# Seven row gathers ahead and nine behind the first jobs, and scale columns read through a register instead of tables

## The reference, cut to what matters

```python
def _L0_xattn_ref(hidden_states, token_ids, Wg, Wu, Wd):
    expert_ids = jnp.minimum(tid // tokens_per_expert, E - 1)
    for e in range(E):
        g = jax.nn.silu(jnp.einsum('bsd,fd->bsf', hidden_states, Wg[e]))
        u = jnp.einsum('bsd,fd->bsf', hidden_states, Wu[e])
        y = jnp.einsum('bsf,df->bsd', g * u, Wd[e])
        out = jnp.where((expert_ids == e)[..., None], y, out)
...
x = x + jnp.tanh(g_xattn[0]) * _L0_xattn_ref(_layernorm(x, axis=-1), itok_BxS_13_99985, ctx_2048, ctx_2048, ctx_2048)
x = x + jnp.tanh(g_ffn[0]) * _L0_ffn_ref(_layernorm(x, axis=-1), L0_ffn_weight)
```

## Time and profile before

| | |
|---|---|
| median of 3 runs | 201.29 us (201.24 to 203.76) |
| the profiled execution: its own time | 201.43 us |
| its span | 199.7 us |
| PE busy | 144.3 us, 72% |
| DVE busy | 156.3 us, 78% |
| ACT busy | 112.7 us, 56% |
| POOL busy | 81.8 us, 41% |

### The profile page before, as it was taken

One profiled execution on the slowest core, in us unless ns is written; L12 is line 12 of the kernel. 1 busy time (PEld: TensorE's weight loads), 2 busy tenths in 40 slices (PEclk: granted clock), 3 DMA queues, 4 the chain that ended last, 5 costly groups with the idle time before them and its releaser, 6 DMA issues.

```text
span 199.7 us, 3062 instructions
## 1 busy us (share of the span) xinstructions
PE 144.3 (72%) x723; PEld 69.7 (35%) x727; DVE 156.3 (78%) x351; ACT 112.7 (56%) x166; POOL 81.8 (41%) x117
## 2 busy tenths in 40 slices
PE   0141939998999797999998999999851266566600
PEld 0110424443555343544444445555420223223200
DVE  2876697798758799899989787776686999998820
ACT  2366596887524854688868534233313987666510
POOL 7158787320312344332386673001110023566670
PEclk9999996999999999999999999999997579999985
DMA  0937998200000222111212210000000002132351
GB/s 6 365 113 198 355 408 264 85 2 0 0 3 0 54 56 53 26 39 43 54 26 53 56 26 0 3 0 2 0 5 0 0 0 105 57 153 113 149 208 59
DMA packets 15440, 15.68 MB, mean 79 GB/s; under 512 B 10816, under 2 KB 11328, under 8 KB 15424
## 3 DMA queue, kind: packets, MB, share of 16 engines
q1 hardware_dynamic: 12576, 7.09, 11.8%
q0 software_dynamic: 2560, 8.39, 11.6%
q10 hardware_dynamic: 288, 0.00, 0.1%
HBM read 8.92 MB, written 4.19 MB: 66 GB/s over the span
## 4 chain that ended last, share of the span: by engine, by line
PE 38%; DVE 33%; issue 11%; POOL 7%; ACT 6%; DMA 1%; DVEq 1%; POOLq 0%
PE four_ps L465 10%; PE four_ps L457 10%; PE four_ps L470 9%; DVE w_hi L1044 3%; DVE hT_hi L1052 3%; PE four_ps L498 3%; POOL x L341 3%; PE four_ps L569 2%; DVE bn L880 2%; DVE zT_lo L866 2%; DVE bn L832 2%; DVE x L1056 2%; ACT y L703 2%; DVE z L861 2%; DVE w_lo L824 2%
## 5 line engine op out<-in xcount | busy, mean ns | idle before, releaser
L364 POOL DMA_INDIRECT out<-x,token_of x16 | 19.3, 1208 | 25.4 <-DVE x L1056 22.9
L359 POOL TENSOR_TENSOR rstd<-var,minus_half 128x1 f32<-128x1 f32 x16 | 8.8, 552 | 49.3 <-DVE var L888 49.3
L633 ACT ACTIVATE zT_hi<-four_ps 128x512 f16<-128x512 f32 x19 | 11.3, 595 | 18.9 <-PE four_ps L498 18.9
L457 PE MATMUL four_ps<-w_hi,hT_hi 128*128 x76 | 21.3, 394 | 0.8 <-ACT w_hi L596 0.7
L624 ACT ACTIVATE sg<-four_ps,job_inv_a 128x512 f32<-128x512 f32 x19 | 12.9, 679 | 15.4 <-PE four_ps L470 12.4
L341 POOL DMA_INDIRECT x<-in_x,token_of x16 | 17.4, 1088 | 7.0 <-issue 4.2
L457 PE MATMUL four_ps<-w_hi,zT_hi 128*128 x76 | 19.5, 379 | 0.8 <-ACT zT_hi L633 0.8
L465 PE MATMUL four_ps<-w_lo,hT_hi 128*128 x76 | 19.9, 384 | 0.0
L615 ACT ACTIVATE w<-x,nmr,rstd 128x512 f32<-128x512 f32 x16 | 13.0, 810 | 11.9 <-DVE nmr L894 11.5
L470 PE MATMUL four_ps<-w_hi,zT_lo 128*128 x76 | 19.5, 379 | 0.0
L465 PE MATMUL four_ps<-w_lo,zT_hi 128*128 x76 | 19.5, 379 | 0.0
(11 more groups left out here) (148 smaller groups left out, 293.4 us busy)
## 6 DMA issues: line engine op xcount, KB each, us to landing
w<-in_ctx_t SPq DMA_DIRECT2D x4, 1024.0 KB, 9.4
wf<-in_wf_t SPq DMA_DIRECT2D x1, 512.0 KB, 15.4
x<-in_x,token_of POOLq DMA_INDIRECT x16, 5.9
out<-x,token_of POOLq DMA_INDIRECT x16, 2.9
hT_hi<-h_row SPq DMA_TRANSPOSE x9, 2.3
hT_lo<-h_row SPq DMA_TRANSPOSE x9, 2.3
ids_s<-in_ids SPq DMA_DIRECT2D x1, 8.0 KB, 2.9
g_s<-in_g_x ACTq DMA_DIRECT2D x1, 0.5 KB, 2.7
```

What stands on the lines that cost most here:

```text
L364: pool.indirect_dma_start(out, bass.IndirectOffsetOnAxis(ap=token_of[:, i:i + 1], axis=0), block_of(x1, i), None, bounds_check=T - 1).then ...
L457: pe.matmul(ps, lhs_hi(k), w_block(w_hi, expert, k), start=(k == 0), stop=False)
```

## The change

**POOL.** Before, POOL issues all 16 gathers, with `rstd_first(0)`, `(1)` and `(2)` behind the gathers 4, 7 and 11. Now it issues gathers 0 to 6, with the three roots behind gathers 2, 4 and 6. Gathers 7 to 9, 10 to 12 and 13 to 15 stand behind POOL's part of jobs 1, 2 and 3.

**DVE and ACT.** The tables `job_is`, `job_of`, `job_inv_a` and `job_z_mul` are gone. `z_of` and `silu` now load the job's expert into a register and read the scale column straight from `w_bits` at that address. `job_mul` is filled one column a job by `factor(j)`, which stands behind `add_y(j - 1)`. On DVE `w_scaling(1)` now stands ahead of `shift_first(1)`. On ACT a wait for `jobs_ready` is added where it has long been met.

```diff
+        def scale_of(expert, n):
+
+            return w_bits[:, bass.ds(expert, 1), n].bitcast(F32)
...
-            after_gather = {4: 0, 7: 1, 11: 2}
-            for i in range(TILES):
+            after_gather = {2: 0, 4: 1, 6: 2}
+            for i in range(EARLY):
                 gather(i)
                 if i in after_gather:
                     rstd_first(after_gather[i])
 
             for j in range(1, TILES + E):
                 job(j)
+                for i in range(EARLY + 3 * (j - 1), min(EARLY + 3 * j, TILES)):
+                    gather(i)
...
             def silu(j):
+                expert = act.value_load(job_expert_i[0:1, j:j + 1], min_val=0, max_val=E - 1)
                 act.wait_ge(a_done, j + 1)
-                if isinstance(j, int) and j < E:
-                    act.wait_ge(job_scales, 2 * (j + 1))
-                if not isinstance(j, int) or j > 0:
+                if j < E:
+                    act.wait_ge(w_scales, j + 1)
+                if j > 0:
                     act.wait_ge(z_done, j)
-                act.activation(sg[:, :], a_ps[:, :], ACT.Silu, scale=job_inv_a[:, bass.ds(j, 1)]).then_inc(silu_done, 1)
+                act.activation(sg[:, :], a_ps[:, :], ACT.Silu, scale=scale_of(expert, INV_A)).then_inc(silu_done, 1)
...
-            product_tables(0)
...
+            def factor(j):
+
+                expert = dve.value_load(job_expert_i[0:1, j:j + 1], min_val=0, max_val=E - 1)
+                dve.tensor_tensor(job_mul[:, j:j + 1], mask[:, j:j + 1], scale_of(expert, INV_Y), ALU.mult)\
+                    .then_inc(job_factor, 1)
...
             def z_of(j):
 
+                expert = dve.value_load(job_expert_i[0:1, j:j + 1], min_val=0, max_val=E - 1)
                 dve.wait_ge(silu_done, j + 1)
                 if j > 0:
                     dve.wait_ge(zT_done, j)
-                dve.scalar_tensor_tensor(out=z[:, :], in0=a_ps[:, :], scalar=job_z_mul[:, j:j + 1], in1=sg[:, :],
+                dve.scalar_tensor_tensor(out=z[:, :], in0=a_ps[:, :], scalar=scale_of(expert, Z_MUL), in1=sg[:, :],
                                          op0=ALU.mult, op1=ALU.mult).then_inc(z_done, 1)
...
-                    product_tables(j + 1)
-                    result_table(j + 1)
-                if not fixed or 1 <= j <= JOBS:
+                if 1 <= j <= JOBS:
                     add_y(j - 1)
+                if j < JOBS:
+                    factor(j)
...
             w_low(0, [3])
             var_first(1)
             hT_low(0)
+            w_scaling(1)
             shift_first(1)
-            w_scaling(1)
-            product_tables(1)
             stats_first(2)
```

More of the change, by code:

```diff
@@ L198, in gated_experts_kernel @@
         squares_done, norms_done, norms_read = sem("squares_done"), sem("norms_done"), sem("norms_read")
-        w_scales, job_scales, job_factors = sem("w_scales"), sem("job_scales"), sem("job_factors")
+        w_scales, job_factor = sem("w_scales"), sem("job_factor")
         wf_step, wf_max_done, wf_scaled = sem("wf_step"), sem("wf_max_done"), sem("wf_scaled")
@@ L253, in first_in @@
             return [i for i in (j + 2, j + 3) if 2 < i < TILES and i - (3 if i >= BY_DMA else 2) == j]
+        EARLY = 7
         WF_MAX, WF_ONES, WF_SCALED, WF_GRID, WF_ROUNDED = 5, 7, 8, 9, 10
@@ L618, in silu @@
             def silu(j):
+                expert = act.value_load(job_expert_i[0:1, j:j + 1], min_val=0, max_val=E - 1)
                 act.wait_ge(a_done, j + 1)
-                if isinstance(j, int) and j < E:
-                    act.wait_ge(job_scales, 2 * (j + 1))
-                if not isinstance(j, int) or j > 0:
+                if j < E:
+                    act.wait_ge(w_scales, j + 1)
+                if j > 0:
                     act.wait_ge(z_done, j)
-                act.activation(sg[:, :], a_ps[:, :], ACT.Silu, scale=job_inv_a[:, bass.ds(j, 1)]).then_inc(silu_done, 1)
+                act.activation(sg[:, :], a_ps[:, :], ACT.Silu, scale=scale_of(expert, INV_A)).then_inc(silu_done, 1)
                 if z_on_pool(j):
-                    act.activation(az[:, :], a_ps[:, :], ACT.Copy, scale=job_z_mul[:, bass.ds(j, 1)])\
+                    act.activation(az[:, :], a_ps[:, :], ACT.Copy, scale=scale_of(expert, Z_MUL))\
                         .then_inc(az_done, 1)
@@ L675, in _ @@
             norm_first(0)
+            act.wait_ge(jobs_ready, 1)
             squares(1, range(1, K))
@@ L797, in _ @@
             w_scaling(0)
[L798 to L806, removed]
-            def product_tables(e):
-                if e > 0:
-                    dve.wait_ge(job_scales, 2 * e)
-                add_expert(job_inv_a, job_is, e, INV_A).then_inc(job_scales, 1)
-                add_expert(job_z_mul, job_is, e, Z_MUL).then_inc(job_scales, 1)
-            def result_table(e):
-                if e > 0:
-                    dve.wait_ge(job_factors, e)
-                add_expert(job_mul, job_of, e, INV_Y).then_inc(job_factors, 1)
-            product_tables(0)
             def w_low(e, chunks=range(K)):
@@ L870, in add_y @@
                 tile = dve.value_load(job_tile_i[0:1, bass.ds(j, 1)], min_val=0, max_val=TILES - 1)
+                dve.wait_ge(job_factor, j + 1)
                 dve.wait_ge(y_done, j + 1)
@@ L937, in masks @@
                 routed(dve.tensor_scalar(mask[:, :], mask[:, :], tg[:, 0:1], None, ALU.mult))
-                routed(dve.tensor_tensor(job_of[:, :, :], job_is[:, :, :],
-                                         mask[:, :].unsqueeze(1).to_broadcast([P, E, JOBS]), ALU.mult))
-                result_table(0)
-                result_table(1)
             def job(j):
```

4 lines of the change are left out of this document (removed).

## The result

The changed kernel takes 207.79 us in the median of 4 runs (206.22 to 208.53). The kernel before took 201.94 us beside it (201.24 to 203.76, 4 runs). The ratio is 1.0265, with a 95% interval from 1.017 to 1.036: slower by 2.65%. The interval shows that the change is slower; whether it is so by more than 2%, it leaves open. The forecast was 204.9 us with a range of 201.8 to 206.6, so the time lies 1.2 us above the range. The profiled execution took 208.53 us, with a span of 206.5 us.

A forecast was written before the change was run, and what follows sets the result against it. Bound taken: front hand-overs between engines, a DVE and POOL loop at 80 to 97 us, PE at 115 to 150 us. Sum: 201.43 - 1.6 + 4.0 + 0.4 + 0.2 + 0.6 = 205.0, forecast 204.9 us, range 201.8 to 206.6.

The forecast's parts named there:

- the load ahead of z: DVE, jobs 6 to 10: z follows var by about 0.87 us instead of 0.09, 5 x 0.8 = 4.0 us slower.
- the front gain: From 19 to 33 us: earlier roots bring nmr, h, w_hi and job 0's z 1.6 us earlier, bounds 0.5 to 2.0.
- the product: DVE, factor's one-column product: 0.08 us a job in jobs 4 to 10 without job 7, 0.5 us in all.
- jobs 11 to 13: DVE: nmr's wait for POOL's root uses up the late z, leaving 0.2 us each in jobs 11 and 12, 0 from 13.
- w_scaling later than thought: Front, DVE: root 1 or w_scaling coming later than thought would cut the gain to its lower bound, 0.5 us.
- the clock in `up(1)`: PE, front: idle time shrinks to about 3.0 us, so the same fall to 1.2 GHz is expected, costing 1.7 us as before.
- rival 2: PE's clock does not fall in up(1) because its idle time is shorter: 1.7 us less, 203.2 us; chance 0.13.
- this loop: Loop through DVE and POOL from z to the next z, said to set the pace in jobs 8 and 9, 5.72 us.
- jobs 4 and 5: DVE: z waits for silu longer than the load, so only the address step counts, 0.1 us each.
- ScalarE's loads: ACT: its 19 register loads run under work without waits, ahead of a wait for PE; cost 0.
- the late gathers: POOL: nine gathers fit its idle time behind jobs 1 to 3, overrunning under 1 us behind job 3; nobody waits.
- Rival 3: Slower by over 2%: loads before z are the long kind, 0.55 us, or front gives only 0.5 us; 206.2 us; chance 0.2.

The follow-up runs named there:

- The two experiments on the load: Changed kernel, next job's expert loaded once behind factor(j), shared by z_of: 201.98 us, 0.9962; kernel before plus an unused load ahead of z's wait: 204.58 us, 1.0128.
- the norm first: Changed kernel with shift_first(1) moved back ahead of w_scaling(1) on DVE: 205.72 us, ratio 1.0177.
- the trace with the fillers: Changed kernel with three extra matmuls, results unused, ahead of the transposes of z in jobs 5 to 12: 208.04 us, ratio 1.0248.
- With the load behind `factor`: Changed kernel with the expert of job j + 1 loaded once behind factor(j), shared by factor and z_of: 201.98 us, ratio 0.9962.
- the kernel with the load added: Kernel before with one unused register load of the job's expert added in z_of ahead of its wait: 204.58 us, ratio 1.0128.

## Why the prediction was wrong

The direction was right, and so were the place and price of the load ahead of z. Two steps failed: the fall of TensorE's clock at job 8, which had no term (1.68 us), and the front gain (0.69 us for 1.6). With the front alone the sum made for the profiled execution would have been 205.9 us, inside the range; with the fall it is 207.6, outside. The median was 2.9 us above the forecast (207.79 for 204.9), and the profiled execution 3.5 us above the sum made for it (208.53 for 205.0).

**Right: the load of z.** "0.8 us more, all of it in the loop, with DVE standing idle": z followed var by 0.85 us, with 0.70 of it idle, and the period of jobs 9 to 11 is 6.50 for 5.72. Jobs 6 to 10 lost 6.07 us in all; without the fall of the clock that is 4.4 us, where load and product together had 4.0 and 0.3 (the product's 0.5 is for six jobs, two of them 4 and 5). The two experiments on the load bear out both its place and its price.

**Right in sum, wrong in place: jobs 11 to 13.** I gave jobs 11 and 12 0.2 us each and job 13 none. They showed 0.76, 0.09 and -0.49, together 0.36 for 0.4. The wait for the root that was to absorb the late z is one that lies behind job 11's z, so it helps from job 12 on.

**Wrong: front gain, 1.6 us.** It was 0.69. The step that failed is "nmr 1 comes at 22.2 and h of tile 1 at 22.3, and w_hi of expert 1 follows h on ACT at 23.0". They came at 23.05, 23.25 and 23.97. My own times already had h behind w_bits and w_hi behind h. I took that for free because it was still 1.6 us better than before, and did not ask what the norm first would have given: there h lies in ScalarE's wait, and here it pushes w_hi back by its length. Of the 0.97 us by which w_hi was late against my steps, w_bits brought 0.64 (its end 22.74 for 22.1). That is the lateness that nmr 0 already had (17.74 for 17.1): root 0 started at 16.69 for 16.4 and took 1.01 us for 0.59, beside w_lo. The other 0.3 us lie between w_bits and h of tile 1, 0.51 us where I had 0.2. In this order every such lateness goes on to h and w_hi. With the norm first w_bits started at the same 22.52, w_hi at 22.77, and the front gain was 1.87 us; so the order alone cost 1.18 us, and without it the forecast gain would have been there. The 0.69 lies within the bounds of 0.5 to 2.0 that I had given, and "w_scaling later than thought" was named for the lower one.

**Right, but with more at stake than told: the clock in `up(1)`.** It fell as before, so rival 2 did not come. I had argued from idle time shrinking "by 0.2 us only". It shrank to 2.04, with `up(0)` running slowly, and the fall came all the same. In the trace with the fillers it was 3.28 us at the same front, so I did not have the idle time in hand. All five traces with POOL's new order and the norm first keep the clock there, with 1.13 to 1.97 us of idle time, and all five with `w_scaling(1)` first lose it. In the change that fall is worth 2.85 - 1.18 = 1.67 us at job 1.

**Wrong, with no term: a second fall.** "PE shows a new wait for z ahead of its transposes" stands in the prediction, and "whatever is put into this loop lengthens each job by its full length" is all that it was to cost. No rival had TensorE's clock fall in jobs 5 to 8. It cost 1.68 us at job 8. What leads to it lies in terms that I did have: the idle time ahead of the transposes, 1.36 and 1.00 us before, grew by my own 0.8 us a job to about 2. I had asked what the idle time in the front would do, and not what the new idle time would.

**Too small: jobs 4 and 5.** I gave 0.2 us, 0.1 for factor's load and two products of 0.08, some 0.46. The transposes went from 0.64 us early (job 4) to 0.10 late (job 5), 0.74 us. Behind the product of `factor` in job 4 nmr comes only at 60.07, 0.32 us of it idle by "issue", and zT_lo, var and h follow it. With the load behind `factor`, nmr comes 0.20 us behind the product and no idle time is shown; jobs 4 and 5 lose 0.37 us there. So 0.3 of it belongs to where the loads stand; I can't say which instruction in the queue holds nmr.

**Right: ScalarE's loads and the late gathers.** The last gather is issued at 55.35 us, and nobody waits for one.

The terms add up: 205.0 forecast, + 0.9 for the front, + 0.3 for jobs 4 and 5, + 1.7 for the second fall, is 207.9 us. The 0.6 us left over lie behind job 13: 0.1 up to the transposes of job 18, 0.2 in the stage behind them and 0.3 around the span.

Rival 3 named the right side. Its first reason was wrong: the loads of z are not the long kind (median 305 ns, one of 16 at 555). Its second, a front that gives only 0.5 us, came near with 0.69. The floor of about 600 ns for such a load, which the prediction cites from the Trainium skill, page "DMA: Bandwidth & Descriptors", section "Latency and other measured facts", is not what these loads take either.

## What to carry to other kernels

A register load takes only 0.3 us, but with what follows it in the queue it cost 0.63 us a job here, 0.78 with the column read at its address, where the queue reached it just behind a wait in the loop that sets the pace. Put it where nothing waits for it, a whole job ahead where the address is known early; here 0.15 us a job were left.

When a step is to move across another, ask of both engines downstream whether the step still fits into their wait, with the measured end of the wait and a margin. Read idle time that is added to TensorE as a risk of its own: see which idle stretches of the trace are followed by the lower clock, and which new ones grow to that size.

The best version by its median takes over POOL's order of gathers and roots alone, keeps the tables, and leaves the norm ahead of `w_scaling(1)`: 199.03 us, 0.9802 of the kernel before.

## What the hardware showed that I had not expected

- TensorE's clock and its idle time ahead of the transposes of z, up to job 18, over all twelve traces: of 12 waits of 2.0 to 3.3 us, nine were followed by a stretch at 1.2 GHz, three of them at once and the others 0.7 to 1.2 us later, and three were not (the changed kernel's 2.10 us at job 5, and 2.08 and 2.09 at job 7 in two others). None of the waits of 1.0 to 1.97 us was.
- The same fall is not worth the same everywhere. In the kernel with the load added, whose front is that of the kernel before (w_hi at 24.60 and the transposes at 28.74 in both), `up(0)` ran slowly, TensorE was idle 1.71 us for 3.22, and the clock held in `up(1)`: 1.2 us earlier at job 1 (36.20 for 37.40), but only 0.23 at job 2 (45.34 for 45.57). With POOL's old order something else was late next.
- A root of one column on GpSimd took 1.01 us beside VectorE's w_lo, and 0.58 without it.
- The last stage takes 56.2 to 58.8 us with the same instructions, by how often TensorE's clock falls in it. That is as much as the differences that were to be measured.
